# Reordering the attention-and-experts stage of an audio tower on one Trainium2 core

## The reference, cut to what matters

```python
# h is (32, 92, 128)
# layer 1: attention over a window of K = 7 tokens, 16 heads of 8
x = layernorm(h)
q, k, v = split(x @ qkv_w.T + qkv_b); q = q * SCALE
attn = softmax(sum over d of q[l] * k[ni(l) + o] + rpb, over o = 0..6)
h = h + (sum over o of attn[o] * v[ni(l) + o]) @ proj_w.T + proj_b
# layer 2: six experts (128 -> 341 -> 128), all computed, weighted for each sequence
x = layernorm(h)
w = top-2 of softmax(mean over tokens(x) @ router_w.T), mapped to six expert weights
h = h + sum over e of w[e] * (gelu(x @ W1[e] + b1[e]) @ W2[e] + b2[e])
```

## Time and profile before

| what | us |
|---|---|
| timed runs, median (lowest to highest) | 826.03 (824.40 to 826.21) |
| profiled execution, own time | 829.29 |
| its span, first to last instruction | 827.5 |
| busy in the span: PE / DVE / ACT / POOL | 630.4 / 622.2 / 519.1 / 277.2 |

### The profile page before, as it was taken

How to read it: one execution, slowest core, us unless ns; L and a number is a source line. 1 busy time by engine, 2 the same in 40 slices (tenths; PEclk the granted TensorE clock), 3 DMA queues, 4 the chain that set the end, 5 groups by cost and what they waited for, 6 DMA issues and landing times.

```text
span 827.5 us, 10897 instructions
## 1 busy us (share of the span) xinstructions
PE 630.4 (76%) x3102; PEld 476.3 (58%) x3103; DVE 622.2 (75%) x1289; ACT 519.1 (63%) x822; POOL 277.2 (33%) x312
## 2 busy tenths in 40 slices
PE   6998751744729164469788799977999999999997
PEld 3564651744619164465555689744566666666565
DVE  1688597999999999999886122268588898896853
ACT  0489999999898998993233134253276466465442
POOL 0464000000000000000487144316346666664642
PEclk9998876968768595879677799999599999999999
DMA  5381043354444555440612366210000000000000
GB/s 180 112 281 59 1 86 59 71 98 91 73 86 86 91 104 100 82 73 6 220 35 70 89 173 189 80 54 1 1 1 4 6 11 6 5 10 7 5 10 18
DMA packets 26383, 56.50 MB, mean 68 GB/s; under 512 B 4203, under 2 KB 15572, under 8 KB 25860
## 3 DMA queue, kind: packets, MB, share of 16 engines
q0 software_dynamic: 5728, 24.56, 15.8%
q1 hardware_dynamic: 19848, 30.80, 12.1%
q10 hardware_dynamic: 764, 0.62, 0.2%
HBM read 29.91 MB, written 10.17 MB: 48 GB/s over the span
## 4 chain that ended last, share of the span: by engine, by line
PE 36%; DVE 27%; issue 15%; ACT 10%; POOL 5%; DMA 3%; POOLq 1%; SPq 1%; DVEq 0%; ACTq 0%
PE psum L2110 6%; DVE s_R L1270 4%; PE psum L1794 4%; DVE s_R L1283 4%; PE psum L2097 3%; POOL x_sorted L686 3%; PE psum L2025 2%; DVE s_R L1294 2%; PE psum L2033 2%; PE psum L2200 2%; DVE s_R L1275 2%; PE psum L2099 2%; PE psum L1892 2%; PE psum L2098 2%; PE psum L1894 2%
## 5 line engine op out<-in xcount | busy, mean ns | idle before, releaser
L1892 PE MATMUL psum<-s_xn_lo,s_split_hi 128*128 128x368 f32 x256 | 94.8, 370 | 136.6 <-ACT s_R L911 133.6
L1892 PEld LDWEIGHTS psum<-s_xn_lo,s_split_hi 128*128 128x128 f32 x256 | 54.7, 214 | 141.1 <-ACT s_R L911 136.3
L671 POOL DMA_DIRECT2D s_xnfm<-s_R x14 | 17.1, 1219 | 259.0 <-DVE s_R L1294 259.0
L1052 ACT ACTIVATE s_R<-psum,s_cols 128x368 f32<-128x368 f32 x96 | 50.3, 565 | 71.6 <-PE psum L2099 71.4
L1289 DVE TENSOR_TENSOR_SCAN s_R<-s_R 128x2944 f32<-128x2944 f32 x15 | 94.4, 6292 | 0.7
L2110 PE MATMUL psum<-s_R 128*128 128x368 f32 x256 | 93.1, 495 | 0.0
L1893 PE MATMUL psum<-s_xn_hi,s_split_lo 128*128 128x368 f32 x256 | 91.8, 358 | 0.0
L1894 PE MATMUL psum<-s_xn_hi,s_split_hi 128*128 128x368 f32 x256 | 91.6, 358 | 0.0
L730 POOL TENSOR_TENSOR s_R<-s_R 128x368 f32<-128x368 f32 x47 | 54.0, 1148 | 38.6 <-DVE s_R L1583 19.3
L767 POOL TENSOR_TENSOR s_R<-s_R 128x368 f32<-128x368 f32 x48 | 46.6, 970 | 58.5 <-DVE s_R L1719 57.8
L918 ACT ACTIVATE s_R<-psum,s_cols 128x736 f32<-128x736 f32 x64 | 55.9, 875 | 13.8 <-PE psum L1894 9.8
(11 more groups left out here) (262 smaller groups left out, 1619.9 us busy)
## 6 DMA issues: line engine op xcount, KB each, us to landing
s_xnfm<-s_R POOLq DMA_DIRECT2D x14, 1472.0 KB, 10.5
s_R<-in_w SPq DMA_DIRECT2D x28, 256.0 KB
s_R<-in_xg SPq DMA_DIRECT2D x7, 744.0 KB, 4.1
x_sorted<-in_x_init SPq DMA_DIRECT2D x1, 5082.0 KB
s_wBC<-in_wBC SPq DMA_DIRECT2D x8, 256.0 KB, 2.8
s_R<-in_v SPq DMA_DIRECT2D x2, 1024.0 KB
s_R<-x_sorted SPq DMA_DIRECT2D x28, 66.0 KB
s_R<-in_w SPq DMA_DIRECT2D x1, 1536.0 KB, 6.5
```

The lines of the kernel that those rows point to most:

```text
L1892: pe.matmul(bank(c), w_hi[:, s, u, k, :], xn_lo[:, a:b], start=True, stop=False)
```

## The change

The last stage's orders are rewritten on all four engines; no arithmetic is changed.

- FFN: the four rest tiles of the first layer stand behind the first three experts, the rests' second layer behind the first layer of experts 3 and 4. The units are numbered in this order (UNITS: 0, 1, rests, 2, 3, 4, 5), so which unit waits for which changes: the second layer of expert 4 waits for `weigh_expert` of expert 2, that of expert 5 for that of expert 3, and that of expert 3 for `rest_out`.
- PE: `qkv_of(c + 1)` stands at the end of period c, followed only by the second layer of expert 1. The spreads go out as (0, 1), (2, 3) and (4, 5, 6); the last group waits for offset 3. `fill_pause` is gone. `shares_fm` stands behind the first layer of expert 5 and the second layer of expert 4.
- DVE: `first_experts(c + 1)` stands behind `shares_rest(c)`, and its statistics, now `experts_stats`, behind offset 0; `residual_stats` is cut into `residual` and `stream_stats`, with `scores_out` in between; `weigh_rest` is second in the period; the experts 2 to 5 are weighed behind `shares`, behind `first_experts`, behind offset 1 and behind offset 3.
- ACT: `normed_e(c + 1)` stands behind the first two GELUs of the new chunk, `rest_out` between exponential and the load of the GELU table, `qkv_out(c + 1)` at the end.
- POOL: `rstd_e(c + 1)` stands in front of the first addition of `weighted_sum(c)`, the additions of experts 4 and 5 between those of the offsets.

The other lines follow from the new numbers (`weigh_expert`, `rest_out` and `ffn` use `unit`, `gelus` waits by it, `result_last` waits for expert 5 in place of the rests).

```diff
@@ -497,21 +497,28 @@
-FFN = ([(1, e, j) for e in (0, 1, 2) for j in range(FT)]
-       + [(2, e, j) for e in (0, 1) for j in range(FT)]
-       + [(1, 3, 0), (1, 3, 1)] + [(1, NE, r) for r in range(NR)]
-       + [(1, 4, 0), (1, 4, 1)] + [(2, e, j) for e in (2, 3) for j in range(FT)]
-       + [(1, 5, 0), (1, 5, 1)] + [(2, e, j) for e in (4, 5) for j in range(FT)]
-       + [(2, NE, r) for r in range(NR)])
+def pair(layer, *es):
+    return [(layer, e, j) for e in es for j in range(FT)]
+def rest_of(layer):
+    return [(layer, NE, r) for r in range(NR)]
+FFN = (pair(1, 0, 1, 2) + rest_of(1) + pair(2, 0, 1)
+       + pair(1, 3, 4) + rest_of(2) + pair(2, 2, 3) + pair(1, 5) + pair(2, 4, 5))
+UNITS = (0, 1, NE, 2, 3, 4, 5)
 ORDER1 = [(e, j) for layer, e, j in FFN if layer == 1]
...
+def unit(f, e):
+    return f * NU + UNITS.index(e)
 def added(g):
...
-def unit_out(eng, f, e):
+def unit_out(eng, g):
+    f, e = g // NU, UNITS[g % NU]
     if e == NE:
...
@@ -759,35 +766,41 @@
-    def weighted_sum(c, after_second):
-        for o in range(1, K):
+    def weighted_sum(c, *offsets):
+        for o in offsets:
             pool.wait_ge(pb_free, c * K + o + 1)
...
             pool.tensor_tensor(pv[:, c % 2], pv[:, c % 2], pv_t[:, o % 2], ALU.add).then_inc(pv_add, 1)
-            if o == 2:
-                after_second()
...
     for c in range(NCH + 2):
-        add_expert(c - 3, NE)
+        att = c < NCH
         if 1 <= c <= NCH:
             projection_bias(c - 1)
+        add_unit(c - 2, 1)
+        if 1 <= c <= NCH:
+            rstd_f(c - 1)
+        add_unit(c - 2, 2)
+        add_unit(c - 2, 3)
+        add_unit(c - 2, 4)
         if c + 1 < NCH:
             rstd_e(c + 1)
-        add_expert(c - 2, 1)
+        if att:
+            weighted_sum(c, 1)
+        add_unit(c - 2, 5)
+        if att:
+            weighted_sum(c, 2)
         if 1 <= c <= NCH:
-            rstd_f(c - 1)
-        add_expert(c - 2, 2)
-        add_expert(c - 2, 3)
-        add_expert(c - 2, 4)
-        add_expert(c - 2, 5)
-        if c < NCH:
-            weighted_sum(c, lambda: second_share(c - 1) if c else None)
-        elif c == NCH:
             second_share(c - 1)
+        if att:
+            weighted_sum(c, 3)
+        if c <= NCH:
+            add_unit(c - 2, 6)
+        if att:
+            weighted_sum(c, 4, 5, 6)
     stage_end(pool, 5)
...
@@ -1070,11 +1078,8 @@
         load_table(ACT.Exp, 0)
-        if c + 1 < NCH:
-            normed_e(c + 1)
         act.wait_ge(sub_done, c + 1)
         act.activation(P_tm[:, c % 2], P_tm[:, c % 2], ACT.Exp).then_inc(exp_done, 1)
-        load_table(ACT.Gelu, 1)
...
+    qkv_out(0)
+    act.wait_ge(wF_ready, 8 * 16)
+    act.activation(spread_r, spread, ACT.Copy).then_inc(spread_ready, 1)
+    act.activation(v1_hi[:, :, :], v1, ACT.Copy).then_inc(v1_hi_ready, 1)
     for c in range(NCH + 2):
-        if c < NCH:
-            qkv_out(c)
-        if c == 0:
-            act.wait_ge(wF_ready, 8 * 16)
-            act.activation(spread_r, spread, ACT.Copy).then_inc(spread_ready, 1)
-            act.activation(v1_hi[:, :, :], v1, ACT.Copy).then_inc(v1_hi_ready, 1)
-        gelus(c - 2, 14, 16)
-        gelus(c - 2, 16, 18)
+        gelus(c - 2, 14, 18)
         if c < NCH:
             exponential(c)
-        gelus(c - 2, 22, 24)
+        rest_out(c - 2)
+        if c < NCH:
+            load_table(ACT.Gelu, 1)
         if 1 <= c <= NCH:
...
             shares_out(c)
+        gelus(c - 2, 26, 28)
         if 1 <= c <= NCH:
             stream_hi(c - 1)
-        if c >= NCH:
-            rest_out(c - 2)
-        gelus(c - 1, 0, 6)
-        if c < NCH:
-            rest_out(c - 2)
-        gelus(c - 1, 6, 12)
+        gelus(c - 1, 0, 2)
+        if c + 1 < NCH:
+            normed_e(c + 1)
+        gelus(c - 1, 2, 8)
         if c + 1 < NCH:
             norm_copies(act, nE, c % 2, c + 1, (7, 7))
-        gelus(c - 1, 12, 14)
+        gelus(c - 1, 8, 10)
+        if c + 1 < NCH:
+            qkv_out(c + 1)
     stage_end(act, 5)
...
@@ -1720,38 +1729,38 @@
     first_experts(0)
+    experts_stats(0)
     for c in range(NCH + 2):
...
         tail = 0 <= f < NCH
+        more = c + 1 < NCH
         if 0 <= f - 1:
             expert_weights(f - 1)
-        weigh_expert(f - 1, 0)
-        weigh_expert(f - 1, 1)
-        if 0 <= f - 1 and not att:
-            weigh_rest(f - 1)
-        if c + 1 < NCH:
-            first_experts(c + 1)
+        weigh_rest(f - 1)
         if att:
...
             dve.tensor_tensor(v1_lo[:, :, :], v1, v1_hi[:, :, :].bitcast(f32), ALU.subtract).then_inc(v1_split, 1)
-        store_chunk(c - 3)
         if tail:
-            residual_stats(f)
+            residual(f)
+        weigh_expert(f - 1, 0)
+        weigh_expert(f - 1, 1)
         if att:
             scores_out(c)
+        if tail:
+            stream_stats(f)
+        if att:
+            scores_less_max(c)
+        store_chunk(c - 3)
+        if att:
+            shares(c)
         weigh_expert(f - 1, 2)
         if att:
-            scores_less_max(c)
+            shares_rest(c)
+        if more:
+            first_experts(c + 1)
         weigh_expert(f - 1, 3)
-        if att:
-            shares(c)
-        weigh_expert(f - 1, 4)
-        if att:
-            weigh_rest(f - 1)
-            shares_rest(c)
-        weigh_expert(f - 1, 5)
         for o in range(K):
...
                     stream_sums(f)
-            if o == 1 and tail:
-                router_largest(f)
+                if more:
+                    experts_stats(c + 1)
+            if o == 1:
+                weigh_expert(f - 1, 4)
+                if tail:
+                    router_largest(f)
             if o == 2 and tail:
...
                     router_second(f)
+                weigh_expert(f - 1, 5)
             if o == 4 and tail:
...
@@ -2180,9 +2194,8 @@
-    def spread_out(c, o):
-        if o % 2:
-            return
+    def spread_out(c, o, *more):
+        two = (o,) + more
         if o == 0:
...
         else:
-            pe.wait_ge(pb_free, c * K + min(o + 1, K - 1) - 2)
-        two = range(o, min(o + 2, K))
+            pe.wait_ge(pb_free, c * K + two[-1] - 2)
         for P, last in ((P_lo, False), (P_hi, True)):
...
@@ -2211,72 +2223,60 @@
+    qkv_of(0)
     for c in range(NCH + 2):
...
         tail = 0 <= f < NCH
-        if att:
-            qkv_of(c)
-        ffn(f - 1, 14, 16)
-        ffn(f - 1, 16, 18)
         if tail:
...
         result_tm(c - 3)
+        ffn(f - 1, 14, 18)
         if att:
...
             scores_tm(c)
-        ffn(f - 1, 20, 22)
+        ffn(f - 1, 20, 26)
         if c < 2:
             keep_busy(8)
-        ffn(f - 1, 22, 26)
+        ffn(f - 1, 26, 30)
         if att:
-            if c >= 2:
-                fill_pause(1)
             shares_fm(c)
...
             keep_busy(1)
-        ffn(f - 1, 26, 28)
         if tail:
...
             pe.wait_ge(v1_split, 1)
-        for o in range(K):
-            if att:
-                spread_out(c, o)
-            if c == 0:
-                keep_busy(1, 2 * L)
-            if not att:
-                if o == 0:
-                    ffn(f - 1, 28, NF)
-                else:
-                    ffn(f, 2 * o - 2, 2 * o)
-            elif 1 <= o <= 3:
-                if o == 1:
-                    ffn(f - 1, 28, 30)
-                    ffn(f, 0, 1)
-                    if tail:
-                        router_logits(f)
-                    ffn(f, 1, 2)
-                else:
-                    ffn(f, 2 * o - 2, 2 * o)
-            elif o == 4:
-                ffn(f - 1, 30, NF)
-            elif o == 5:
-                ffn(f, 6, 8)
-            elif o == 6:
-                if tail:
-                    router_spread(f)
-                ffn(f, 8, 12)
-            if o == 1 and tail and not att:
-                router_logits(f)
+        if att:
+            spread_out(c, 0, 1)
+        if c == 0:
+            keep_busy(2, 2 * L)
+        ffn(f - 1, 30, NF)
+        ffn(f, 0, 1)
+        if tail:
+            router_logits(f)
+        ffn(f, 1, 2)
+        if att:
+            spread_out(c, 2, 3)
+        if c == 0:
+            keep_busy(2, 2 * L)
+        ffn(f, 2, 4)
+        if att:
+            spread_out(c, 4, 5, 6)
+        if c == 0:
+            keep_busy(3, 2 * L)
+        ffn(f, 4, 8)
         if c + 1 < NCH:
-            pe.wait_ge(pb_free, c * K + K - 1)
+            pe.wait_ge(pb_free, c * K + 5)
             norm_transposes(pe, nE, c % 2, c + 1, (7, 7))
+        ffn(f, 8, 12)
+        if tail:
+            router_spread(f)
+        if c + 1 < NCH:
+            qkv_of(c + 1)
         ffn(f, 12, 14)
-        if tail and not att:
-            router_spread(f)
     result_last()
...
```

More of the change, by code:

```diff
@@ L717, in _, with add_unit @@
             stage_end(pool, 4)
-            def add_expert(f, e):
+            def add_unit(f, k):
                 if not 0 <= f < NCH:
                     return
-                g = f * NU + e
```

(34 more changed lines are left out.)

1 line of the change is left out of this document (removed).

## The result

The changed kernel takes 840.58 us (median of 4 runs, 836.69 to 841.21) against 826.12 for the kernel before on the same chip: a ratio of 1.016, 95% interval 1.0135 to 1.0185. It is 1.6% slower, inside the forecast range and 2.4 us under the forecast. Its profiled execution has a span of 839.0 (own time 840.85), 11.5 more than the 827.5 of before.

A forecast was written before the change was run, and what follows sets the result against it. The prediction took one loop of waits between PE, DVE and ACT as the bound. Loop +8, start +1, end 0 and clock +8 on 826 gave 843 us; forecast case 836 to 851, whole range 829 to 855.

The forecast's parts named there:

- Loop: Period through turned scores, shares, first spread and offset 3: 1.6 us longer, +8 over five periods (chunks 2 to 6).
- C: From the shares to the first spread: 3.4 us in place of 2.69, 0.7 more.
- D: From the first spread to the end of offset 3, on DVE: 7.8 us in place of 5.40, 2.4 more.
- A: From the end of offset 3 to the next turned scores, PE's long queue: 16.0 us, 1.5 less than before.
- Start: Chunks 0 and 1: additions start later, behind rstd_e, but chunk 1 no longer begins with first_experts; +1, between -2 and +3.
- End: Last periods, without next chunk or first_experts, PE's work in both orders: 0, between -3 and +3.
- Clock: PE's stretch between expert 4 and expert 5: two falls to half clock, 4.1 us each, +8 together.
- the stretch that was named: PE between expert 4 and expert 5, with only shares_fm, the stream's turn and the first spread: 3.3 us, clock falls expected.
- No fall: Rival: no fall of PE's clock, the longer loop alone, 826 + 9 = 835 us; chance 0.28.
- PE's queue alone: Rival: PE's own work sets the period, 28.5 against 30.88 us, so 814, if DVE comes 4 us earlier; chance 0.12.

The follow-up runs named there:

- fillers: Changed kernel plus three matmuls nothing reads in PE's waits, one ahead of the first spread, two ahead of the last: 836.89 us, ratio 1.0132.
- The rows at the front: Changed kernel with first_experts and its statistics at the front of DVE's period, and rstd_e moved with them on GpSimd: 828.43 us, ratio 1.0031.
- the early shares: Changed kernel with the turn of the shares (shares_fm) put in front of the second layer of expert 4: 831.31 us, ratio 1.0077.
- the two splits of the last spread: Changed kernel with offset 6 spread behind expert 2's first layer: 840.97 us; the same with normalized rows behind expert 1's GELUs: 842.01 us.
- expert 3 first: Changed kernel with the weighing of expert 3 put ahead of first_experts on DVE: 845.25 us, ratio 1.0228.

## Why the prediction was right, and where not

The direction and the mechanism of the loop were right, its four terms to about 0.2 us. The total came close by luck in part: the clock was put 6.8 too high, the start 2.1 too low and the end 0.9 too high, and the timed medians, for which the forecast was 2.4 too high, lie 14.5 apart where the profiled runs lie 11.5 apart.

- *Loop, predicted +8.* Without falls 32.59 (fillers) against 30.95, five times: +8.2. C and D are the terms that the prediction gave. The rows at the front take away the growth of D, the early shares that of C and 0.4 of D.
- *A.* PE's queue was summed to 16.0; it is 16.16, and PE's busy time in A fell by the 1.4 that was summed, from 17.13 to 15.70. What the prediction did not say is that the shorter queue needed the expert rows gone from the front of DVE's period. In the kernel before DVE works, but for a pause of 0.21, from 631.91, where its expert rows stand, to the scores, and PE waits 0.31 for it: DVE lay just behind PE. Rows at the front again give 17.58 with the short queue; `qkv_of` at the front does not. No run undid the new order of the experts' units alone. The 1.4 us that DVE was to have in hand ahead of the scores were used up: in chunk 5 of the changed kernel its products end at 707.66, just as PE begins the scores.
- *Start, predicted +1 (-2 to +3).* +3.1. D of chunk 0 is 6.12 in place of 3.48, because the expert rows and statistics of chunk 1 stand in it; the prediction counted only the late additions. With the rows at the front D is 3.47.
- *End, predicted 0.* -0.9.
- *Clock, predicted +8, the step that failed.* Two falls came in the stretch that was named, behind the first spread, and that is the number expected. But each cost 0.3, not 4.1: they lasted 3.4 us, and PE, late by the half clock, only waited less for DVE at the last spread (0.34 in place of 1.56 in chunk 5, at 727.22). I had doubled 4.45 us of PE's work and then some. Two more came around the last spread, which the prediction had not named, and cost 2.4 and 1.4 in A, where PE idles for only 0.5 in all. Together with what chunk 2 carries over from chunk 1 they are 167.88 - 5 x 32.59 = 4.9. And the kernel before pays too: its fall of chunk 1, from 583.24 to 600.30, makes the period of chunk 2 34.72, 3.8 over the others, of which the changed kernel has 0.4 left. Net +1.2.

Sum: 3.1 + 8.2 + 1.2 - 0.9 = 11.6, against 11.5 measured and 17 predicted.

The Trainium skill, "TensorE: Matmul & The Clock Gate", section "HAM oscillation — how this bites in real kernels", blames waits of PE. By that rule the prediction had set "no falls". There were falls, with no single wait over 1.56 in chunks 2 to 6; but filling the waits ended them, so the trace agrees with waits as the cause, and not with the prediction's reading of it by the longest single wait.

*The rivals.* "No fall" (835) is the kernel with fillers, 836.9. "PE's queue alone" (814) was put at DVE coming 4 us earlier at the turn of the shares; 1.2 out of C and 2.1 out of D brought 818.

## What to carry to other kernels

Cut a software pipeline at the points where its chain changes engine, add the stretches, and price each moved instruction in the stretch where it lands. Nine runs here moved instructions; five were forecast within 1.5 us that way, one of them by luck in part and three from stretches already measured in other runs, and four missed by 4.7 to 8.2: the two splits of the last spread, expert 3 first, and `qkv_of` back. Moving DVE's additions to H was free where GpSimd idled too (1.12) and dear beside its additions (3.26). Before praising a part of a change, undo that part alone: the move of query, key and value gained nothing.

## What the runs showed of the hardware

The same four additions to H took 1.12 to 1.13 beside an idle GpSimd, 1.83 beside one addition of it and 3.26 beside three. GpSimd loses as well: its reciprocal root, 1.01 alone, took 2.50 when it met DVE's weighing of the rests, in the run with the rows at the front:

```profile
725.78 2.50 POOL L746 TENSOR_TENSOR s_rs<-s_pa,s_mhalf 92x4 f32<-92x4 f32 x1
```

The Trainium skill, "SBUF — State Buffer", section "SBUF: two separate sides", has DVE instructions with two inputs in SBUF, or in a mode that uses two ports, and GpSimd's take turns at one port pair, each for its whole length. The additions above agree. DVE's L1567 on 4x6 elements, which has one tensor input and took 0.28 in the kernel before (657.97), took 1.82 in the changed kernel (662.81): it ends at 664.63, with GpSimd's second addition beside it (663.65 to 664.61). That looks like the same turn-taking; no run here shows in which mode L1567 runs.

The other surprise was that falls of the clock of 3.4 us come in a loop whose PE never waits for as long as 2 us; why some periods have one and their like do not stays open.
